# Conv gate, attention and mixture-of-experts layer on one core: the attention steps reordered

## What is computed

```python
x = x + conv_gate(group_norm(x))                  # per image and channel: one factor
t = tokens(x)                                     # [8, 256, 512]
t = t + attention(layer_norm(t))                  # 16 heads of 32, tanh soft cap, causal
t = t + moe(layer_norm(t))                        # 8 experts, top 2, and a shared expert

# attention: q, k, v = x @ w.T; s = 30 * tanh(q k^T / sqrt(32) / 30); softmax(masked s) @ v; @ w_o.T
# moe: shared = silu(x @ sg) * (x @ su) @ sd; routed experts of the two best gates per token, weighted
```

## Time and profile before

| what | value |
|---|---|
| median of three executions | 743.72 us |
| profiled execution, its own time | 743.5 us |
| its span | 741.7 us |
| PE busy | 651.9 us (88% of the span) |
| PE weight loads busy | 527.1 us (71%) |
| DVE, ACT, POOL busy | 387.6, 281.3, 284.9 us |
| mean granted TensorE clock | 0.990 |

### The profile page before, as it was taken

One profiled execution on the slowest core, in us unless ns is written; L12 is line 12 of the kernel. 1 busy time (PEld: TensorE's weight loads), 2 busy tenths in 40 slices (PEclk: granted clock), 3 DMA queues, 4 the chain that ended last, 5 costly groups with the idle time before them and its releaser, 6 DMA issues.

```text
span 741.7 us, 13486 instructions
## 1 busy us (share of the span) xinstructions
PE 651.9 (88%) x4866; PEld 527.1 (71%) x4867; DVE 387.6 (52%) x895; ACT 281.3 (38%) x498; POOL 284.9 (38%) x329
## 2 busy tenths in 40 slices
PE   0214989999999999999899999999799999999992
PEld 0213978878787878788689899999567676676761
DVE  7765354746464656463654996233444444444341
ACT  8641263636364545464624223444221211212210
POOL 1330243333333324241421113865354554545534
PEclk9999999999999999999999999999999999999997
DMA  9700000101010101011206433351855556555443
GB/s 312 313 0 0 1 2 1 58 2 57 0 57 0 57 0 57 0 53 34 86 1 257 128 114 115 114 170 43 297 92 107 99 99 111 93 107 101 97 72 42
DMA packets 24642, 62.07 MB, mean 84 GB/s; under 512 B 3041, under 2 KB 7905, under 8 KB 23073
## 3 DMA queue, kind: packets, MB, share of 16 engines
q1 hardware_dynamic: 14768, 41.16, 15.5%
q0 software_dynamic: 9168, 20.45, 15.0%
q10 hardware_dynamic: 672, 0.03, 0.1%
HBM read 38.56 MB, written 23.07 MB: 83 GB/s over the span
## 4 chain that ended last, share of the span: by engine, by line
PE 79%; DVE 10%; issue 3%; DMA 3%; POOL 2%; ACT 1%; SPq 1%; DVEq 0%; POOLq 0%; ACTq 0%
PE scores L1442 25%; PE PS L1442 22%; PE scores L1770 9%; PE PS L1551 5%; PE scores L1689 5%; PE scores L1537 3%; PE PS L1713 2%; PE PS L1502 2%; DMA wd_sb<-in_wd 1%; DVE rden L1114 1%; DMA T<-in_x 1%; PE PS L1761 1%; PE PS L1491 1%; DVE front L957 1%; DVE front L1061 1%
## 5 line engine op out<-in xcount | busy, mean ns | idle before, releaser
L1442 PE MATMUL scores<-xb,sw_h 128*128 128x256 f32 x512 | 93.9, 284 | 0.0
L617 POOL DMA_INDIRECT out_tokens<-yo,dest x36 | 57.1, 1586 | 83.5 <-DMA out_tokens<-yo,dest 80.5
L1442 PEld LDWEIGHTS scores<-xb,sw_h 128*128 128x128 f32 x512 | 80.6, 191 | 2.1 <-issue 0.4
L1442 PE MATMUL PS<-xt_h,w_h 128*128 128x256 f32 x256 | 76.4, 299 | 3.6 <-issue 2.1
L837 ACT ACTIVATE es<-scores 128x256 f32<-128x256 f32 x39 | 15.0, 384 | 160.4 <-PE scores L1442 160.4
L1770 PE MATMUL scores<-wd_sb,ehT 128*128 x156 | 73.6, 594 | 1.7 <-DVE ehT L1402 1.0
L534 POOL TENSOR_SCALAR_AFFINE_SELECT probs<-probs 128x256 f32<-128x256 f32 x128 | 51.3, 428 | 61.9 <-ACT probs L719 61.7
L1442 PE MATMUL PS<-xt_l,w_h 128*128 128x256 f32 x256 | 73.4, 287 | 0.0
L1442 PE MATMUL PS<-xt_h,w_l 128*128 128x256 f32 x256 | 73.3, 286 | 0.0
L1442 PE MATMUL scores<-xb,sw_l 128*128 128x256 f32 x256 | 72.2, 282 | 0.0
L1114 DVE RECIPROCAL rden<-PS 128x256 f32<-128x256 f32 x32 | 56.1, 1755 | 26.7 <-PE PS L1551 26.7
(11 more groups left out here) (285 smaller groups left out, 1458.0 us busy)
## 6 DMA issues: line engine op xcount, KB each, us to landing
wgu_l<-in_wgu SPq DMA_DIRECT2D x8, 1024.0 KB, 6.7
T<-in_x SPq DMA_DIRECT2D x8, 512.0 KB, 7.8
w_in<-in_wqkvo SPq DMA_DIRECT2D x4, 1024.0 KB, 12.2
x_rows<-x SPq DMA_DIRECT2D x8, 512.0 KB, 2.8
x_cols<-x2T SPq DMA_DIRECT2D x8, 512.0 KB, 2.7
xc<-x_cols SPq DMA_DIRECT2D x8, 512.0 KB, 3.3
out_tokens<-T SPq DMA_DIRECT2D x8, 512.0 KB, 7.5
wd_sb<-in_wd SPq DMA_DIRECT2D x8, 512.0 KB, 7.0
```

Of the source, the lines that this page charges most:

```text
L617: pool.indirect_dma_start(out[:, :], bass.IndirectOffsetOnAxis(dest[:, t:t + 1], 0), yo[:, t % 3, :], None, compute_op=ALU.add).then_inc(y ...
L1442: ins = pe.matmul(out, lhs(k, a), rhs(k, b), start=m == 0, stop=m == len(products) - 1)
```

## The change

Four things are changed. No arithmetic changes, and no instruction is added to or taken from the work, but for waits.

1. In the first, mid and late steps PE does `K1` before `head_values(b, 3)`, not behind it; DVE copies it out before `normalise(b, 3)`.
2. `attention_added` takes the statistics of tile 0 between the two additions; those of tile 1 (`added_stats`) now stand behind `xt_low`, ahead of `tile_variance`. In the tail they stand right behind the additions.
3. The last step has a program of its own on PE, DVE, ACT and POOL (`last_step`). OP0 stands behind scores 0 and 1, OP1 behind `head_values(b, 0)`; the gate's transposes behind the first hidden chunk, the gate's partial sums behind the second, and the logits between the tail's OP0 and OP1. On POOL `rstd_of` moves from behind mask 1 to behind mask 3 and `att_low(b, 0)`. On ACT `split_high(0, 0)` moves from the head of the step to behind `soft` 3.
4. PE waits for the late step's V1 to be copied out before `head_values(b, 0)` of the last step, where it waited before its first scores.

```diff
@@ GpSimd
+            def last_step(b):
+                for p in range(4):
+                    mask(b, p)
+                att_low(b, 0)
+                rstd_of(var2_ready, rstd2_ready, b - 1)
+                mask(b, 4)
+                mask(b, 5)
+                att_low(b, 1)
+                mask(b, 6)
+                mask(b, 7)
+                att_low(b, 2)
+                att_low(b, 3)
...
@@ ScalarE
-                if part == "last":
-                    split_high(0, 0)
...
+            def last_step(b):
+                for p in range(4):
+                    soft(b, p)
+                split_high(0, 0)
+
+                act.wait_ge(*filled("last", "OP1", b))
+                att_high(b, 0)
+                soft(b, 4)
+                soft(b, 5)
+                att_high(b, 1)
+                soft(b, 6)
+                soft(b, 7)
+                att_high(b, 2)
+                x2_transposed("last", b)
+                att_high(b, 3)
+                act.wait_ge(x2T_stored, 16 * b)
...
@@ VectorE
-                dve.wait_ge(att_ready, 4 * s if part == "tail" else 4 * s + 2)
+                dve.wait_ge(att_ready, 4 * s + {"tail": 0, "last": 4}.get(part, 2))
...
             def attention_added(part, b, s):
...
+                tile_added(part, b, s, 0)
+                added_stats(part, b, s, 0)
+                tile_added(part, b, s, 1)
+
+            def added_stats(part, b, s, tt):
+                dve.wait_ge(*emptied(part, f"OP{tt}", s))
+                stand_alone(dve)
+                step_of(dve.bn_stats(bn6[:, tt, :], tile_at(b, tt)))
...
                 if has_front:
                     xt_low(part, b + 1, b)
                 if has_back:
+                    added_stats(part, b - 1, b, 1)
                     tile_variance(var2_ready)
...
                     project_out(part, "Q1", b)
+                    project_out(part, "K1", b)
                 normalise(b, 3)
...
+            def last_step(b):
+                tile_added("last", b - 1, b, 0)
+                normalise(b, 0)
+                tile_added("last", b - 1, b, 1)
+                for tt in range(TT):
+                    dve.wait_ge(*emptied("last", f"OP{tt}", b))
+                tile_stats(b - 1)
+                tile_variance(var2_ready)
+                normalise(b, 1)
+                second_out(b - 1)
+                split_low(0, 0)
+                normalise(b, 2)
+                normalise(b, 3)
+                partial_out("last", b - 1, b)
+                hidden_shared(0, 0, True)
+                hidden_shared(0, 1, True)
+                gate_top("last", b - 1, b)
...
@@ TensorE
                 head_values(b, 2, first)
                 if has_front:
                     heads_projection(part, "Q1", b)
...
+                if has_front:
+                    heads_projection(part, "K1", b)
                 head_values(b, 3, first)
                 if has_front:
-                    heads_projection(part, "K1", b)
                     values_projection(part, b, 0)
                     values_projection(part, b, 1)
...
+            def last_step(b):
+
+                for p in (0, 1):
+                    head_scores(b, p, False)
+                pe.wait_ge(att_l_done, 4 * b)
+                out_tile("last", b - 1, b, 0)
+                head_scores(b, 2, False)
+                head_scores(b, 3, False)
+                pe.wait_ge(*emptied("late", "V1", b - 1))
+                head_values(b, 0, False)
+                out_tile("last", b - 1, b, 1)
+                head_scores(b, 4, False)
+                head_scores(b, 5, False)
+                head_values(b, 1, False)
+                head_scores(b, 6, False)
+                head_scores(b, 7, False)
+                head_values(b, 2, False)
+                pe.wait_ge(tanh_done, 8 * b + 7)
+                pe.wait_ge(xb_l_done, 1)
+                hidden_chunk(0, 0, True, 0)
+                gate_transposes("last", b - 1, b)
+                head_values(b, 3, False)
+                hidden_chunk(0, 1, True, 0)
+                gate_partial("last", b)
+
+                pe.wait_ge(att_l_done, 4 * b + 4)
+                out_tile("tail", b, B, 0)
+                gate_logits("last", b - 1, b)
+                out_tile("tail", b, B, 1)
```

More of the change, by code:

```diff
@@ L547, in hidden_low @@
                                    ALU.subtract).then_inc(hl_done, 1)
+            def last_step(b):
[10 more added lines that the diff above has]
+                att_low(b, 3)
+                hidden_low(0, 0)
+                hidden_low(0, 1)
+                rstd_of(var2_ready, rstd2_ready, b)
             def step(b, has_next):
@@ L579, in _ @@
             step(B - 2, False)
-            step(B - 1, False)
+            last_step(B - 1)
             def weight_low(m):
@@ L774, in _ @@
             step("late", B - 2, True, True, False)
-            step("last", B - 1, False, True, False)
+            last_step(B - 1)
             def gated_shared(b, j):
@@ L1142, in gate_top, with tile_added @@
                 dve.wait_ge(dve_step, step_of(dve.tensor_copy(topi[:, bass.ds(b * TT, TT), :], idx8[:, :, :])))
+            def tile_added(part, b, s, tt):
+                dve.wait_ge(*filled(part, f"OP{tt}", s))
+                k, _ = ring(part, f"OP{tt}", s)
+                dve.tensor_tensor(tile_at(b, tt), ring_bank[k], tile_at(b, tt), ALU.add).then_inc(ring_free[k], 1)
             def attention_added(part, b, s):
[L1146 to L1153, removed]
+                tile_added(part, b, s, 0)
[5 more added lines that the diff above has]
+                step_of(dve.bn_stats(bn6[:, tt, :], tile_at(b, tt)))
             def second_out(b):
@@ L1220, in _ @@
             step("late", B - 2, True, True, False)
-            step("last", B - 1, False, True, False)
+            last_step(B - 1)
             attention_added("tail", B - 1, B)
+            added_stats("tail", B - 1, B, 1)
             tile_variance(var2_ready)
@@ L1554, in head_values, with out_tile @@
                 ins.then_inc(pv_done, 1)
+            def out_tile(part, b, s, tt):
+                bank, full = begin(part, f"OP{tt}", s)
+                triple(bank, range(CB), lambda k, a: (att_h, att_l)[a][:, k, tt * P:(tt + 1) * P],
+                       lambda k, a: wslice((w_h, w_l)[a], 3, k, 0, C)).then_inc(full, 1)
             def out_projection(part, b, s):
@@ L1558, in out_projection @@
                 pe.wait_ge(att_l_done, 4 * b + 4)
[L1559 to L1562, removed]
+                out_tile(part, b, s, 0)
+                out_tile(part, b, s, 1)
             def gate_transposes(part, b, s):
@@ L1676, in _ @@
             pe.wait_ge(*emptied("late", "K1", B - 2))
-            pe.wait_ge(*emptied("late", "V1", B - 2))
-            step("last", B - 1, False, True, False)
-            out_projection("tail", B - 1, B)
+            last_step(B - 1)
             def down_chunk(b, j, first):
```

17 lines of the change are left out of this document (removed).

## The result

The changed kernel takes 731.69 us (median of four executions, 730.78 to 731.98) where the kernel before takes 744.06 (four executions in the same session, 743.08 to 745.25). The ratio is 0.9835, with an interval from 0.9818 to 0.9852. The forecast was 733.1. The profiled execution took 731.98 us, its span is 730.2 us, 11.5 less than the span before.

A forecast was written before the change was run, and what follows sets the result against it. PE, busy 88% of the span, was taken to bound the kernel. K1 6.5, statistics 2.5 and last step 1.6 sum to 10.6 us off 743.5: 732.9, median 733.1; own range 732 to 734.5, wide range 730.9 to 736.5.

The forecast's parts named there:

- K1 ahead: Ahead of value group 3: K1 fills PE's wait for `att`, which goes whole in five mid steps; 6.5 us won.
- Nothing late next: Before OP0 of the next step: the later `att` chain of group 3 still ends in time, with 3.6 us in hand.
- K1 does nothing for want of a ring bank: Rival at K1: something else in the ring holds it, so moving it early wins nothing; 739.6 us or no change, chance 0.03.
- the wait moves to OP0: Rival: group 3's wait only moves to OP0 of the next step; 739.6 us if all returned, chance 0.03.
- Statistics early: Ahead of Q0: one statistic between DVE's additions lets `xt_l` start earlier, removing PE's wait in mid and late steps; 2.5 us.
- The last step: New order in the last step, clock falling before group 2: tail ends at 382.6 against 384.20; 1.6 us won.
- The wait ahead of group 0: In the last step: a new wait for mask 1 of 0.5 to 0.6 us, as only one out tile covers the softmax.
- the gap of 2.1 us ahead of group 2: In the last step: group 2 waits for mask 5 until 364.1; PE has 0.9 of work in the 3.0 us before.
- the two cases: Last step's end: 382.6 with the low clock or 381.5 at full clock; 1.6 or 2.7 us won.
- the rival that I gave 0.2: Rival in the last step: the clock stays up; 731.9 to 732.2 us, chance 0.2.
- The port rule: Last step: DVE's `x` in a two-port mode could hold POOL's mask 5 about 1 us, a microsecond above the forecast.
- the wide one: Range of the total with the two cases of the last step included: 730.9 to 736.5 us, holding some 8 in 10.

The follow-up runs named there:

- The two kernels with a later low part: Changed kernel with POOL's last low part of each step but the last done four times (733.67 us) or eight times (753.87 us).
- two of them with filling: Changed kernel plus seven matmuls nobody reads in the last step: 731.77 us; with four, `w_o` low pieces between first-step masks and `xb_l` ahead of `x`: 728.54 us.
- the trace without a fall: Changed kernel with POOL's four low pieces of `w_o` put between the first step's masks, not ahead of them: 729.83 us.

## Why the prediction was right

**K1 ahead.** Right in mechanism and nearly in size: 6.15 against 6.5, by the kernel with K1 alone. The wait was lost whole and came back nowhere. The term lay high because I weighed in the weight loads' side of the wait; PE's next matmul is what counts.

**Nothing late next.** I had 3.6 us in hand before OP0. The two kernels with a later low part put it between 2.5 and 5.7, and by the wait of 1.9 at 5.7, near 3.8. That K1 does nothing for want of a ring bank, and that the wait moves to OP0, are refuted by the same traces.

**Statistics early.** Right: 5 x 0.40 + 0.30 = 2.3 against 2.5. Again the matmul side alone (0.37, and 0.03 of the rest) was the price.

**The last step.** The forecast was made step by step on the clock of the trace before; that clock is ahead of the new trace by 349.25 - 338.97 = 10.28 us. Set so, group 2 was to start at 364.1 and started at 353.91 + 10.28 = 364.2; it was to end at 366.8, and the chunk began at 366.65; the chunk was to end at 370.3 and ended at 370.4; the tail was to end at 382.6 and ended at 382.5. The wait ahead of group 0 was put at 0.5 to 0.6 and is 0.54. The gain was put at 1.6 and is 1.66 with a fall on both sides. One thing inside it was off: the gap of 2.1 us ahead of group 2 is one of 1.05, 0.17 for ACT and 0.88 for POOL. Scores 6 and 7 stand apart, as the second waits for ACT, and each alone took 0.92 (the row at 352.11) where two together take 0.95. The end of the gap, which POOL sets, was right. At full clock the forecast was off by more: it had 1.1 us between the two cases, and it is 0.66, as the chunk waits for an `xb_l` that comes 0.5 later than I had it.

**The clock in the last step.** In the profiled execution it fell where I put it, and this was luck: in the six later traces with the new last step and room at OP0 it did not (two of them with filling), and the rival that I gave 0.2 is what these show: 39.61 in place of 40.27, 0.66 less. The Trainium skill (TensorE: Matmul & The Clock Gate, What's actually happening) ties the clock to how busy the engine has been of late. No row here speaks against that, but the same instructions with the same wait gave 1.00 in one trace and 0.50 in another, so the page and the rows of one trace together give a case, not a forecast.

**The port rule.** In the prediction mask 5 might have been held for the length of `x`. The instructions of masks 4 and 5 took 1.62, as before; they were not held, and `x`, which began 0.3 before they ended, took 1.04. But DVE and POOL stretched each other a little later. These are the rows of the changed kernel:

```profile
354.51 1.76 DVE L1202 TENSOR_TENSOR xb<-xc,xb 128x1024 fp32r<-128x1024 f32 x1
```

```profile
355.82 1.07 POOL L534 TENSOR_SCALAR_AFFINE_SELECT probs<-probs 128x256 f32<-128x256 f32 x2 [0.64 <-ACT probs L731]
```

`xb` began 0.67 before the end of `att_l` (the row at 354.16 above) and took 1.76 us where it took 1.21, 0.55 more; the next mask began 0.45 before the end of `xb` and took 1.07 where a mask takes 0.77, 0.30 more; `att_l` took 1.02 where it takes 0.74 alone. So the later of the two lost most of the time that the earlier one still ran. The page that the prediction cites, the Trainium skill (SBUF — State Buffer, Who interferes with whom), gives the pair of ports to whichever starts first, and mask 5 had started before `x`: by that rule too it was not the mask that would be held, and the prediction's reading of the rule left this out. I had counted `xb` at 1.21. It ended at 356.27 and the chunk began at 356.37, the same 0.10 behind it as in the trace without a fall. So the start of the chunk, which the forecast had from group 2 at a low clock, came out right in part by chance: `xb_l`, later than I had it, was there at the same time.

**The sum.** The pieces measured are 6.15 + 2.3 + 1.66 = 10.1, where I had 10.6. The time came out 1.4 us lower than forecast all the same, since one term was missing on the side of before. The profiled execution of before had a low clock in its first step, the one of after had none:

```profile
95.28 0.86 PE L1597 MATMUL PS<-probs,v 128*32 128x256 f32 x16 [1.92 <-POOL probs L534]
...
100.66 0.86 PE L1597 MATMUL PS<-probs,v 128*32 128x256 f32 x16
```

In the trace before, the same rows stand at 95.58 (1.38 long, behind a wait of 1.90) and 102.55: 6.97 from one to the other against 5.38, that is 1.59 us. The change has no part in it: over all traces with that wait the fall came in five of 12, with the old order and with the new.

Between medians the difference is 12.4, and some 2.3 us of it are more than the waits that went. These look like falls of the clock, which the kernel before has oftener. Of its 31 executions beside the experiments, three took 742.5 or less, with a mean granted clock of 0.991 to 0.993, and 28 took 743.75 or more, with 0.988 to 0.990 (or 0.961 and 0.962 where the stretch at 60 us, below, is recorded as low); with K1 alone four executions of 735.2 to 736.5 have 0.992, two of 738.6 and 739.4 have 0.989 (0.965 in one of the four, with the stretch at 60 us low). Where these falls lie, and why the kernel before has more of them, is not shown. The new last step isn't needed to lose them: K1 alone and the statistics alone keep the old one, with its wait for the gate's transposes, and have won 2.4 and 2.5 beyond their waits all the same. The forecast has nothing on this, so that part of its closeness is chance.

Compared without any fall, before is a span of 739.8, and after is 730.2 - 0.67 or 731.5 - 1.6, about 729.7: 10.1 us, which is what the waits account for.

**The range.** The bounds that the prediction names for its three terms, 6.1 to 7.1, 1.9 to 3.3 and 1 to 2, add up to 9.0 to 12.4, which makes 731.3 to 734.7 and not its own range of 732 to 734.5. The measured 731.69 lies just below the range as stated, and inside the wide one of 730.9 to 736.5.

## What to carry to other kernels

A wait that the chain has in every step is worth its length on the matmul side, if work of that length can be brought ahead of it and the chain behind the moved wait has the room; count the room as carefully as the gain, since past it the wait comes back, here with a low clock on top in four of six steps. When two profiled executions of a kernel differ by a microsecond or two, compare the distances between the same rows of a step before reading anything into the total. Where a wait has several semaphores, the view may name the wrong one: read when each of them was set.

## What the runs showed of the hardware

The granted clock falls behind a thin stretch (waits, with little work of PE between them) in some executions and not in others, with the same program and the same wait. Behind the wait of 1.9 us for a mask in the first step it fell in five of 12 traces and cost 1.6 us; behind OP0's wait of 1.9 in four of six steps, 1.6 too; behind group 1 of the old last step it fell in three of six traces, ahead of group 2 of the new one in one of seven, and cost 0.6 to 0.7; behind the 1.9 us for `x2T` in the old order 3.1, in one trace of two.

The recorded clock did not go with the speed of the work where PE did little. At 60 us, before the attention, the trace of before says 1.00 and that of after 0.50, and eight transposes take 1.97 us in both, where eight take 1.03 in a mid step. The stretch and the transposes, in the trace of after:

```profile
60.00:62.00 2.00, 1.50 (x7) 1.50 (x8) 0.44 (x2) 0.35 (x1) 0.00 (x0) 0.50 0.00 0
```

```profile
60.50 1.97 PE L1537 MATMUL PS<-ident,front 128*128 128x128 f32 x8 [4.86 <-DVE front L1088]
```

So the mean granted clock of 0.962 after against 0.990 before tells of no loss.

DVE and POOL stretched each other where both read and wrote SBUF: `xb` 1.76 for 1.21, `att_l` 1.02 for 0.74, a mask 1.07 for 0.77. The later one lost somewhat less than what was left of the earlier one: 0.55 of 0.67, and 0.30 of 0.45.
